# Layer 0's cross attention in four units of four tiles, with its weights loaded in the layernorm ahead

## The reference, cut to what matters

```python
def _L0_xattn_ref(x, support, attn_mask, qkv_w, proj_w, proj_b):
    wq, wk, wv = (qkv_w[:C], qkv_w[C:2 * C], qkv_w[2 * C:])
    q = jnp.einsum('bnc,dc->bnd', x, wq)
    k = jnp.einsum('bmc,dc->bmd', support, wk)
    v = jnp.einsum('bmc,dc->bmd', support, wv)
    attn = jnp.einsum('bnd,bmd->bnm', q, k) * SCALE
    attn = jax.nn.softmax(attn, axis=-1)
    attn = jnp.where(attn_mask[None, None, :] == 0, 0.0, attn)
    out = jnp.einsum('bnm,bmd->bnd', attn, v)
    out = jnp.swapaxes(out, 1, 2).reshape(B, N, C)
    return jnp.einsum('bnc,dc->bnd', out, proj_w) + proj_b
x = _layernorm(x + _L0_xattn_ref(x, ctx_1024, mask_S2_ik0, ...), axis=-1)
```

## Time and profile before

| | us |
|---|---|
| median of 3 runs | 2767.8 |
| lowest and highest | 2764.31, 2769.44 |
| the profiled execution's own time | 2763.51 |
| its span, first to last instruction | 2761.8 |
| TensorE busy in the span | 2368.4 |
| VectorE busy | 1411.7 |
| ScalarE busy | 1162.0 |
| GpSimd busy | 632.9 |

### The profile page before, as it was taken

The page is one execution under the profiler, slowest core; times in us unless marked ns, Lnnn a source line. Parts: engine busy times, 40 slices in busy tenths (PEclk is TensorE's granted clock), DMA queues, the critical chain, the costliest instruction groups (busy, mean ns, idle before and its releaser), DMA issues. The chain is left out here.

```text
span 2761.8 us, 42785 instructions
## 1 busy us (share of the span) xinstructions
PE 2368.4 (86%) x15752; PEld 1550.3 (56%) x15752; DVE 1411.7 (51%) x3183; ACT 1162.0 (42%) x2044; POOL 632.9 (23%) x850
## 2 busy tenths in 40 slices
PE   1388998999887899959999998689899798499996
PEld 1267754444425599944444434267565443389996
DVE  5725366785454322247887974656455454611114
ACT  6524234565333111134776773332333323434444
POOL 5100042222110023322011001100255410145551
PEclk8769978998988999978999999889999898699998
DMA  5100022220101279942112101022111110378996
GB/s 183 49 15 1 19 48 47 47 48 17 28 10 55 81 266 334 327 125 50 28 26 43 27 2 48 1 66 65 32 29 22 45 26 2 136 277 338 354 347 239
DMA packets 86596, 269.54 MB, mean 98 GB/s; under 512 B 25306, under 2 KB 44242, under 8 KB 70124
## 3 DMA queue, kind: packets, MB, share of 16 engines
q1 hardware_dynamic: 70708, 233.69, 27.3%
q0 software_dynamic: 15680, 33.12, 3.7%
HBM read 207.95 MB, written 23.94 MB: 84 GB/s over the span
## 5 line engine op out<-in xcount | busy, mean ns | idle before, releaser
L1490 DVE TENSOR_REDUCE cmax<-ring 128x1 f32<-128x512 f32 (+3 forms) x896 | 514.5, 625 | 136.5 <-PE ring L1360 70.5
L1475 ACT ACTIVATE prob<-st_ps 128x1024 f32<-128x1024 f32 x448 | 413.8, 933 | 234.1 <-PE st_ps L1352 231.5
L2910 PE MATMUL A<-xbT,w 128*128 128x128 f32 x2512 | 300.9, 276 | 0.3 <-issue 0.3
L2910 PEld LDWEIGHTS A<-xbT,w 128*128 128x128 f32 x2512 | 291.1, 193 | 0.6 <-issue 0.5
L1400 PE MATMUL acc<-prob,v 128*32 128x256 f32 (+2 forms) x3200 | 265.4, 405 | 1.2 <-POOL prob L1293 0.7
L3160 DVE COPY yb<-C 128x256 f32<-128x256 f32 x118 | 50.1, 424 | 283.5 <-PE C L2918 283.5
L2827 POOL DMA_INDIRECT y_rows_dram<-yb,dst x118 | 116.3, 986 | 322.8 <-DVE yb L3160 319.6
L2918 PE MATMUL C<-w,hid 128*128 128x256 f32 x632 | 149.5, 380 | 0.0
L1352 PE MATMUL st_ps<-qst,kst 64*128 64x512 f32 (+3 forms) x560 | 137.5, 489 | 8.4 <-DMA qst<-crow 7.5
L2814 POOL DMA_INDIRECT xb<-x_rows_dram,src x118 | 115.3, 977 | 122.2 <-DVE src L3130 86.9
L1360 PE MATMUL ring<-kst,qst 48*128 48x512 f32 (+3 forms) x560 | 131.2, 402 | 11.2 <-DVE cmax L1490 6.7
(11 more groups left out here) (456 smaller groups left out, 4531.0 us busy)
## 6 DMA issues: line engine op xcount, KB each, us to landing
w<-L3f_W_dram SPq DMA_DIRECT2D x79, 1026.0 KB
w<-L1f_W_dram SPq DMA_DIRECT2D x39, 1536.0 KB
room<-y_rows_dram SPq DMA_DIRECT2D x8, 1024.0 KB, 9.2
kst<-parts SPq DMA_DIRECT2D x120, 64.0 KB, 2.4
qst<-parts SPq DMA_DIRECT2D x120, 64.0 KB, 2.4
gate<-L2f_gates_dram SPq DMA_DIRECT2D x5, 1536.0 KB, 7.3
first<-parts SPq DMA_DIRECT2D x96, 64.0 KB, 2.4
qT<-dense SPq DMA_DIRECT2D x84, 64.0 KB, 2.4
```

The source lines that it names most:

```text
L1475: act.activation(prob[:, step % PROBS, 2 * p:2 * p + 2, 0:n], st_ps[:, p, :, 0:n], ACT.Exp, scale=scale)\
L1490: dve.tensor_reduce(cmax[:, a, t:t + 1, k0 // CH], spot(key)[:, 0:k1 - k0], AX.X, ALU.max)\
L2910: mm = pe.matmul(A[:, j % 2 * 2 + a, f * TB:(f + 1) * TB], up_w(w[:, j % WB], a, k, f), xbT[:, j % 2, k, :], start=(k == 0), stop=(k == KT ...
```

## The change

Three things change.

The loads of wkT, wq and wvT leave the block of `wide_cross`. They are issued by SyncE in the layernorm before it, through `ahead`, into `env.w3`, and the three SBUF tensors of their own are gone. The three loads left are issued in another order, projT last.

The two halves of eight tiles become four units (`UNITS`) of four (`QT`). Scores, transposes and outputs have two buffers each, and the engines' lists are interleaved over the units: TensorE does the scores of unit u+2 and the transposes of unit u+1 ahead of the outputs of unit u. The scores of units 0 and 1 stand ahead of the values. The output banks hold two tiles each and are handed over in pairs.

The probabilities are no longer scaled by the inverse sum. ScalarE applies it at the output copy, as a scale operand per partition. The addition of proj_b to `env.xT` goes from ScalarE to GpSimd, behind the last scores.

The core of the diff, with removed lines where they are not plain from the code above:

```diff
+        row_norm(nc, env, turned(env, lambda k, t: h_out[:, k, t * P:(t + 1) * P]), ahead=ahead)
...
+    QT = HT // 2
+    UNITS = NT // QT
+    wkT, wq, wvT = env.w3[:, 0], env.w3[:, 1], env.w3[:, 2]
...
-                sp.dma_start(wkT[:, :, :], dram.wkT.rearrange("(k p) n -> p k n", p=P)).then_inc(s.wk_loaded, 16)
-                sp.dma_start(wq[:, :, :], dram.wq.rearrange("(k p) n -> p k n", p=P)).then_inc(s.wq_loaded, 16)
-                sp.dma_start(wvT[:, :, :], dram.wvT.rearrange("(k p) n -> p k n", p=P)).then_inc(s.wv_loaded, 16)
-                sp.dma_start(projT[:, :, :], dram.projT.rearrange("(k p) n -> p k n", p=P)).then_inc(s.loaded, 16)
-                sp.dma_start(proj_b[:, :], dram.proj_b).then_inc(s.loaded, 16)
-                sp.dma_start(mask_i[:, :], dram.mask.rearrange("(m a) -> m a", a=1)).then_inc(s.loaded, 16)
+                sp.dma_start(proj_b[:, :], dram.proj_b).then_inc(s.proj_loaded, 16)
+                sp.dma_start(mask_i[:, :], dram.mask.rearrange("(m a) -> m a", a=1)).then_inc(s.proj_loaded, 16)
+                sp.dma_start(projT[:, :, :], dram.projT.rearrange("(k p) n -> p k n", p=P)).then_inc(s.proj_loaded, 16)
+
+            @block.gpsimd
+            def _(pool):
+                pool.wait_ge(s.proj_loaded, 48)
+                pool.wait_ge(s.score_ready, UNITS)
+                for k in range(KT):
+                    pool.tensor_scalar(env.xT[:, k, :], env.xT[:, k, :], proj_b[:, k:k + 1], None, ALU.add).then_inc(s.moved, 1)
...
+                def scores(u):
+                    if u >= 2:
+                        pe.wait_ge(s.sub_done, u - 1)
+                    b = u * QT // HT
+                    for t in range(QT):
+                        tok = (u * QT + t) * P
+                        for k in range(KT):
+                            mm = pe.matmul(score_ps[:, u % 2, t, 0:M], env.xT[:, k, tok:tok + P], qkT[:, k, b * M:(b + 1) * M],
+                                           start=(k == 0), stop=(k == KT - 1), skip_group_check=True)
+                    mm.then_inc(s.score_ready, 1)
+
+                def turn(u):
+                    pe.wait_ge(s.exp_done, u + 1)
+                    if u >= 2:
+                        pe.wait_ge(s.turned_kept, u - 1)
+                    for t in range(QT):
+                        mm = pe.transpose(turn_ps[0:M, u % 2, t, :], pr[:, u, t, :], env.ident[:, :])
+                    mm.then_inc(s.turned, 1)
+
+                def outputs(u):
+                    pe.wait_ge(s.turned_kept, u + 1)
+                    pe.wait_ge(s.v_kept, 1)
+                    for t in range(QT):
+                        i = u * QT + t
+                        n = i // 2
+                        if n >= 2 and i % 2 == 0:
+                            pe.wait_ge(s.out_kept, 2 * (n - 1))
+                        mm = pe.matmul(out_ps[:, n % 2, i % 2, :], prT[:, u, t, :], v[:, u * QT // HT, :], start=True, stop=True, skip_group_check=True)
+                        if i % 2:
+                            mm.then_inc(s.out_ready, 1)
+
+                pe.wait_ge(loaded, 48)
...
+                scores(0)
+                scores(1)
...
+                turn(0)
+                for u in range(UNITS):
+                    if u + 2 < UNITS:
+                        scores(u + 2)
+                    if u + 1 < UNITS:
+                        turn(u + 1)
+                    outputs(u)
...
-                act.wait_ge(s.loaded, 48)
-                act.wait_ge(s.score_ready, NB)
-                for k in range(KT):
-                    act.activation(env.xT[:, k, :], env.xT[:, k, :], ACT.Identity, bias=proj_b[:, k:k + 1])
...
+                def exponent(u):
+                    act.wait_ge(s.sub_done, u + 1)
+                    act.activation(pr[:, u], sc[:, u % 2], ACT.Exp, scale=scale).then_inc(s.exp_done, 1)
+
+                def keep_outputs(u):
+                    act.wait_ge(s.inv_done, u + 1)
+                    for t in range(QT):
+                        i = u * QT + t
+                        n = i // 2
+                        act.wait_ge(s.out_ready, n + 1)
+                        act.activation(o[:, i, :], out_ps[:, n % 2, i % 2, :], ACT.Copy, scale=inv[:, u, t:t + 1]).then_inc(s.out_kept, 1)
+
+                exponent(0)
+                exponent(1)
+                for u in range(UNITS):
+                    if u + 2 < UNITS:
+                        exponent(u + 2)
+                    keep_outputs(u)
...
+                def soften(u):
+                    dve.wait_ge(s.score_ready, u + 1)
+                    dve.tensor_reduce(rowmax[:, u, :], score_ps[:, u % 2, :, 0:M], AX.X, ALU.max).then_inc(s.max_done, 1)
+                    dve.wait_ge(s.max_done, u + 1)
+                    if u >= 2:
+                        dve.wait_ge(s.exp_done, u - 1)
+                    dve.tensor_tensor(sc[:, u % 2], score_ps[:, u % 2, :, 0:M], last(rowmax[:, u, :], M), ALU.subtract)                       .then_inc(s.sub_done, 1)
+
+                def weigh(u):
+                    dve.wait_ge(s.exp_done, u + 1)
+                    dve.tensor_reduce(rowsum[:, u, :], pr[:, u], AX.X, ALU.add).then_inc(s.sum_done, 1)
+                    dve.wait_ge(s.sum_done, u + 1)
+                    dve.reciprocal(inv[:, u, :], rowsum[:, u, :]).then_inc(s.inv_done, 1)
+
+                def keep_turned(u):
+                    dve.wait_ge(s.turned, u + 1)
+                    dve.tensor_copy(prT[:, u].rearrange("m t p -> m (t p)"), turn_ps[0:M, u % 2].rearrange("m t p -> m (t p)"))                       .then_inc(s.turned_kept, 1)
...
-                dve.wait_ge(s.loaded, 48)
+                dve.wait_ge(s.proj_loaded, 48)
                 dve.tensor_scalar(keep[:, :], mask_i[:, :], 0, None, ALU.not_equal).then_inc(s.kept, 1)
+                soften(0)
+                soften(1)
+                weigh(0)
...
-                    dve.wait_ge(s.inv_done, b + 1)
-                    dve.tensor_tensor(pr[:, b], pr[:, b], last(inv[:, b, :], M), ALU.mult).then_inc(s.prob_done, 1)
...
+                keep_turned(0)
+                for u in range(UNITS):
+                    if u + 2 < UNITS:
+                        soften(u + 2)
+                    if u + 1 < UNITS:
+                        weigh(u + 1)
+                        keep_turned(u + 1)
...
+                    def wide_weights(sp):
+                        for i, n in enumerate(("wkT", "wq", "wvT")):
+                            sp.dma_start(env.w3[:, i], d["L0x_" + n].rearrange("(k p) n -> p k n", p=P)).then_inc(wide_loaded, 16)
+
+                    min_gru(nc, env, group("L0a_"), dict(group("L0f_"), x=d["in_x"], ctxT=d["in_ctxT"]), fold, wide_weights)
+                    wide_cross(nc, env, space("L0x_"), wide_loaded)
```

More of the change, by code:

```diff
@@ L664, in folding, with min_gru @@
                  first_down=keep_first_down, second_down=keep_second_down)
-def min_gru(nc, env, dram, weights, fold):
+def min_gru(nc, env, dram, weights, fold, ahead):
     with ExitStack() as st:
@@ L849, in _ @@
                 pe.wait_ge(s.key_kept, 1)
-                pe.wait_ge(s.wq_loaded, 16)
                 for m in range(KT):
@@ L862, in _ @@
                 mm.then_inc(s.v_ready, 1)
-                for b in range(NB):
-                    if b:
-                        pe.wait_ge(s.sub_done, b)
-                    for t in range(HT):
-                        tok = (b * HT + t) * P
-                        for k in range(KT):
-                            mm = pe.matmul(score_ps[:, t, 0:M], env.xT[:, k, tok:tok + P], qkT[:, k, b * M:(b + 1) * M],
-                                           start=(k == 0), stop=(k == KT - 1))
-                    mm.then_inc(s.score_ready, 1)
@@ L872, in _ @@
-                for b in range(NB):
-                    pe.wait_ge(s.prob_done, b + 1)
-                    if b:
-                        pe.wait_ge(s.turned_kept, b)
-                    for t in range(HT):
-                        mm = pe.transpose(turn_ps[0:M, t // (HT // 2), t % (HT // 2), :], pr[:, b, t, :], env.ident[:, :])
-                    mm.then_inc(s.turned, 1)
-                    pe.wait_ge(s.turned_kept, b + 1)
-                    pe.wait_ge(s.v_kept, 1)
-                    for t in range(HT):
-                        i = b * HT + t
-                        if i >= 2:
-                            pe.wait_ge(s.out_kept, i - 1)
-                        pe.matmul(out_ps[:, i % 2, 0:D], prT[:, b, t, :], v[:, b, :], start=True, stop=True)\
-                          .then_inc(s.out_ready, 1)
+                turn(0)
@@ L888, in _ @@
+                for u in range(UNITS):
[4 more added lines that the diff above has]
+                    outputs(u)
             @block.scalar
             def _(act):
-                for b in range(NB):
-                    act.wait_ge(s.sub_done, b + 1)
-                    act.activation(pr[:, b], sc[:, :, :], ACT.Exp, scale=scale).then_inc(s.exp_done, 1)
-                act.wait_ge(s.loaded, 48)
```

(20 more changed lines are left out.)

37 lines of the change are left out of this document (13 added, 24 removed).

## The result

| | before | after |
|---|---|---|
| median of 8 runs, us | 2766.06 | 2750.32 |
| lowest and highest | 2758.13, 2770.14 | 2743.89, 2760.41 |
| profiled execution, its span | 2763.51, 2761.8 | 2746.89, 2745.2 |
| the stage, first DMA issue to the next stage's ScalarE table load | 136.57 to 185.17, 48.6 | 134.94 to 168.21, 33.3 |

What follows compares the result with a forecast made beforehand. TensorE bounds the stage, with holes and mostly at 1.2 GHz: 48.6 us becomes 40.9, or 36.0 with 6.8 us at 2.4 GHz. Gaining 12.6 from 2763.5 gives 2750.9, 2755 on the median's scale, range 2746 to 2762.

Steps and rivals of the forecast that it cites:

- rival A: Clock stays high after the values and into the next layernorm: stage 30.5 us, 20.2 us gained, total 2747.6; chance 25%.
- Weights ahead: Stage start: loading wkT, wq and wvT in the layernorm before lets TensorE start at 0 instead of 2.9 us.
- TensorE's holes: The old order left TensorE idle 10.75 us; in the new one at 1.2 GHz it never stops after 5.99 us.
- The scores at 1.2 GHz: Each unit's scores take 3.0 us at 1.2 GHz; units 0 and 1 end at 12.0 us into the stage.
- The clock: TensorE rises to 2.4 GHz by the values' end for 6.8 us, making the gain 12.6 us instead of 7.7.
- The output copy: ScalarE's copy with scale takes 0.55 us a tile, bounds 0.38 and 0.72, hidden behind TensorE at 1.2 GHz.
- GpSimd: Additions of proj_b behind the last scores take 3 us each, bounds 2.0 and 7.07, hidden under turns and outputs.
- VectorE beside GpSimd: After the last scores, VectorE's PSUM-fed work such as unit 3's subtract isn't blocked by GpSimd; counted as nothing.
- C: GpSimd holds up VectorE's subtract of unit 3: stage 51.8 us, 3.2 us slower, total 2771; chance 8%.
- Scaling of pr: Ahead of the transposes, two VectorE instructions of 0.80 us go, leaving only the exponential late for them.

Runs made afterwards that it cites:

- e3: Changed kernel with the value product ahead of the scores of units 0 and 1: stage 41.3 us, total 2765.3 us (1 run).
- e4: Kernel before the change with TensorE's holes filled by unused products: stage 39.9 us, total 2742.5 us (1 run).
- e5: The same kernel as e3 once more, on another chip: stage 31.8 us, total 2748.7 us (4 runs), ratio to the kernel before 0.9956.
- e7: Changed kernel with units undone to two halves, keeping early loads, inverse sum at output copy and proj_b on GpSimd: stage 42.6 us, total 2755.3 us (1 run).
- e9: e7 with TensorE's holes filled by unused products: stage 36.8 us, total 2751.9 us (1 run).
- e1: Changed kernel with GpSimd's addition of proj_b cut in two by batch: stage 30.5 us, total 2742.6 us (6 runs), ratio to the kernel before 0.9927.
- e10: Changed kernel with probabilities scaled by VectorE again and no scale at the output copy: stage 43.5 us, total 2757.8 us (1 run).
- e11: e10 with the addition of proj_b left out, so GpSimd is idle: stage 44.5 us, total 2756.7 us (1 run).
- e8: e1 with the value product first, into the output banks, and four unused products last: stage 25.7 us, total 2739.2 us (6 runs), ratio 0.9914.
- e12: e8 without the four unused products behind the last outputs: stage 25.6 us, total 2740.4 us (4 runs), ratio to the kernel before 0.9902.

## Why the prediction was right, step by step

The total was right: 12.6 us forecast, 14.7 measured by the ratio, 2750.3 in a range of 2746 to 2762. The way there was a mixture of the forecast and rival A: the stage took 33.3 us, midway between the forecast's 36.0 and A's 30.5. Four terms were mis-sized, and that they came out this close is partly luck: the clock gave more than I allowed, and the scores at 1.2 GHz and GpSimd's tail took some of it back.

- *Weights ahead*, 2.9 us: the keys start 0.06 us into the stage. Right.
- *TensorE's holes*: none above 0.57 us up to the outputs of unit 3. Right. That the holes' 10.75 us come back, less what the clock and the tail take, was the right frame.
- *The scores at 1.2 GHz* take 3.45 us a unit, not the 3.0 that I took from 22 records in 4.4 us; units 0 and 1 ended 12.9 us into the stage instead of 12.0. At this rate e3, all at 1.2 GHz, took 41.3 us, where my sum for such a stage was 40.9.
- *The clock* was the largest mis-sized term. I let it stay up for 6.8 us, as before; it stayed 17. I had read the low clock during the outputs as a property of the outputs. It is not: in after, e4 and e5 they ran at 2.4 GHz throughout. Nor do they hold it: in e7 and e9 it fell in their midst. e4 and e9 gained 8.7 and 5.8 us when the holes were filled, in one execution each, so holes have a part in its fall; they aren't all of it, as e9 shows. The Trainium skill (TensorE: Matmul & The Clock Gate, Part 1, "What's actually happening") has sustained activity release the clock; e5 and the changed kernel agree, and e3, busy but for two holes of 0.57 us and low for 41 us, doesn't.
- *The output copy* with a scale takes 0.41 us a tile (1.64 for four), not 0.55: my row had a bias operand and another function. Its bound of 0.38 was nearer.
- *GpSimd*: 5.45 us per addition, not 3, inside the range of 2.0 to 7.07. I had said that it decides from 6.7 us at the low clock and, in A, that it must be done within 8.6; it took 10.9 and set the end, 4.0 us late. So A came out at 33.3 instead of 30.5; in e1, without this tail, the stage was 30.5. The low start of the layernorm, which A had high, has another reason, for in e1 it was low as well. The Trainium skill (GPSIMD Engine Reference, "4.1 Engine selection") calls one-input work roughly line-rate; here it is 2.7 ns a column against ScalarE's 0.95 for the same addition (3.88 us for 4096).
- *VectorE beside GpSimd*: the subtract of unit 3 took 0.48 us at 157.35. C is out, though the additions were over the 5.4 us each that it asked for: the stage wanted no VectorE instruction of the kind that is slowed. The Trainium skill (SBUF — State Buffer, "Who interferes with whom") has a VectorE instruction with two SBUF inputs contend with a GpSimd instruction that reads SBUF, and spares one with at most one SBUF input; the traces agree, for the subtract with its scores from PSUM kept its 0.48 us, and the scaling with two SBUF inputs took 2.61 us in e10.
- *Scaling of pr*: I put its removal down as two instructions of 0.80 us. Inside the new order it is what lets softmax fit under a unit's scores; with it the stage is 10 us longer (e10), somewhat more by holes than by the clock, and 11 longer without GpSimd's addition (e11), mostly by the clock.

From 48.6 to 33.3, as far as the single profiles split it: 6.0 early loads and no scaling (e7, of which about 1 is its second spell of high clock), 5.8 filled holes and the clock that comes with them (e9), 3.5 units less GpSimd's tail. One kernel's stage was 33.3 and 34.2 in two profiles, and another's 41.3 and 31.8, so each share is uncertain by this much. What stays open is why the clock rises at the values in one execution and not in another of the same kernel, and what lets it fall where no hole stands before it.

## What to carry to other kernels

Where TensorE sets the pace at 1.2 GHz, first ask whether holes let its clock fall: filling them with unused products is a test of a few lines, and in one execution it gave 8.7 us of the stage, more than half of the 15.3 of the rewrite. Repeat such a profile before believing it. Put gapless work that depends on nothing first in a stage: in e8 and e12 the clock was up over 9 us earlier than in the changed kernel. When work moves to a slower engine so as to be hidden, compare its time with what is left behind its wait, at the fastest clock of the others.

## What the runs showed of the hardware

- GpSimd's f32 addition of a per-partition operand takes 5.45 us for 128x2048 and 2.85 for 128x1024.
- A VectorE product of 128x308 with both inputs in SBUF takes 2.6 to 2.9 us instead of 0.48 when GpSimd runs such an addition (e10, e11), and ends before the addition does; PSUM-fed subtracts keep their 0.48.
- Three loads of 256 KB issued one behind the other landed 2.9, 3.2 and 4.2 us behind their issues (before).
- One kernel's stage took 41.3 us in one execution (e3) and 31.8 in another on another chip (e5), with the same instructions at different clocks.
